# A transformer layer on one core: queries and keys turned in the q, k, v stage

## The reference

```python
mod = (silu(c) @ wmod).reshape(4, 6, 1, -1)        # sa, ca, ga, sb, cb, gb
h = layernorm(x) * (1 + ca) + sa
q = (layernorm(h) * qn_g + qn_b) @ Wq + bq          # k, v: the same with kvn_*, Wkv, bkv
q, k = rotary(q * hd**-0.25, |h|), rotary(k * hd**-0.25, |h|)
qn, kn = layernorm(q, ln_g, ln_b), layernorm(k, ln_g, ln_b)   # over the 32 channels of a head
w = softmax(causal(qn @ kn.T / sqrt(hd)))
x = x + ga * ((w @ v) @ Wo + bo)
x = x + gb * ffn(layernorm(x) * (1 + cb) + sb)
```

## Time and profile before

| | |
|---|---|
| three runs | 2335.0, 2336.63, 2336.87 us; median 2336.63 |
| the profiled execution | 2335.2 us, of which its span is 2333.5 |
| PE, DVE, ACT, POOL busy over the span | 93%, 51%, 34%, 32% |
| q, k, v stage | up to 399.7 us |
| attention | 399.7 to about 1100 us |
| PE's clock | full but for the starts of stages; mean 0.60 from 380 to 400 us, 0.5 at 400 to 460 us |
| chain that ended last | PE 45% of the span, all in the feed-forward stage |

### The profile page before, as it was taken

One profiled execution on the slowest core, in us unless ns is written; L12 is line 12 of the kernel. 1 busy time (PEld: TensorE's weight loads), 2 busy tenths in 40 slices (PEclk: granted clock), 3 DMA queues, 4 the chain that ended last, 5 costly groups with the idle time before them and its releaser, 6 DMA issues. The chain is left out here.

```text
span 2333.5 us, 36753 instructions
## 1 busy us (share of the span) xinstructions
PE 2167.5 (93%) x14056; PEld 1684.2 (72%) x14056; DVE 1190.7 (51%) x2747; ACT 788.2 (34%) x1575; POOL 758.3 (32%) x668
## 2 busy tenths in 40 slices
PE   6989995599999999998687999999999999999998
PEld 3777773377777777775465888888888888888887
DVE  5999996667667667663697122222211222222212
ACT  3333331066665666565355111111111111111111
POOL 2667776121222222222771222222222222222221
PEclk8999997599999999999898999999999999999999
DMA  6132322647575756641896112121111212121111
GB/s 235 58 105 90 108 94 102 154 108 167 127 164 127 165 139 152 152 103 39 261 308 216 54 55 68 50 68 36 60 64 50 68 55 68 50 73 50 53 33 54
DMA packets 164851, 243.99 MB, mean 105 GB/s; under 512 B 20604, under 2 KB 87292, under 8 KB 164184
## 3 DMA queue, kind: packets, MB, share of 16 engines
q1 hardware_dynamic: 160504, 229.27, 34.2%
q0 software_dynamic: 3136, 9.46, 1.3%
q10 hardware_dynamic: 1056, 3.15, 0.3%
HBM read 131.69 MB, written 59.26 MB: 82 GB/s over the span
## 5 line engine op out<-in xcount | busy, mean ns | idle before, releaser
L1363 DVE TENSOR_TENSOR f_gu<-f_psU,f_silu 128x512 f32<-128x512 f32 x128 | 88.5, 692 | 712.3 <-PE f_psU L1430 712.3
L999 ACT ACTIVATE b_probT<-b_psB 128x512 f32<-128x512 f32 (+1 forms) x640 | 316.8, 554 | 170.8 <-PE b_psB L863 168.5
L932 DVE TENSOR_REDUCE b_top<-b_psA 128x2 f32<-128x1024 f32 (+2 forms) x320 | 284.7, 902 | 153.8 <-PE b_psA L840 153.7
L1319 POOL TENSOR_SCALAR f_wd_hi<-f_wd 128x512 fp32r<-128x512 f32 x128 | 83.6, 653 | 823.8 <-PE f_psD L1415 776.2
L1339 ACT ACTIVATE f_silu<-f_psG 128x512 f32<-128x512 f32 x128 | 76.6, 598 | 504.4 <-PE f_psG L1430 504.4
L863 PEld LDWEIGHTS b_psB<-b_stack 98*128 98x128 f32 x1280 | 183.6, 190 | 73.1 <-issue 51.6
L863 PE MATMUL b_psB<-b_stack 98*128 98x256 f32 (+1 forms) x1280 | 218.3, 291 | 6.1 <-ACT b_probT L999 3.9
L1428 PE MATMUL f_psG<-f_hT_hi,w_hi 128*128 128x512 f32 x512 | 200.4, 391 | 11.4 <-DVE f_hT_lo L1357 11.4
L840 PE MATMUL b_psA<-b_stack 96*128 96x512 f32 (+3 forms) x768 | 184.7, 370 | 23.2 <-DMA b_stack<-b_halves 18.0
L1334 ACT ACTIVATE f_gu_hi<-f_gu 128x512 fp32r<-128x512 f32 x128 | 80.9, 632 | 364.5 <-DVE f_gu L1363 364.5
L1429 PE MATMUL f_psG<-f_hT_hi,w_lo 128*128 128x512 f32 x512 | 200.1, 391 | 0.0
(11 more groups left out here) (172 smaller groups left out, 4010.4 us busy)
## 6 DMA issues: line engine op xcount, KB each, us to landing
b_stack<-b_halves SPq DMA_DIRECT2D x192, 256.0 KB, 4.8
f_wd<-in_wd_t SPq DMA_DIRECT2D x128, 256.0 KB, 2.6
qkv_d<-a_t SPq DMA_DIRECT2D x32, 512.0 KB, 2.7
b_land<-qkv_d SPq DMA_DIRECT2D x32, 512.0 KB, 4.2
a_x<-in_x SPq DMA_DIRECT2D x32, 256.0 KB, 3.3
qkv_d<-a_v SPq DMA_DIRECT2D x32, 256.0 KB, 3.1
b_v<-qkv_d SPq DMA_DIRECT2D x16, 512.0 KB, 6.3
att_d<-b_acc SPq DMA_DIRECT2D x16, 512.0 KB, 3.2
```

The lines of the kernel that those rows point to most:

```text
L932: last = dve.tensor_reduce(into, tile[:, :, col:col + whole_blocks * P], AX.X, ALU.max, negate=True)
L999: act.activation(probT[:, (NW * n + w) % PROBS, j, 0:width], psB[:, i % BANKS, 0:width], ACT.Exp).then_inc(s["expd"], 1)
```

## The change

- After `norm_heads`, PE transposes a tile's queries and keys in the q, k, v stage (`turn_qk`, four blocks of 128 by 128 each, into `psT`), ACT scales and shifts them (`out_qk`), and SP stores them turned. `v` has two buffers in place of four, and is stored by itself. The eight small loads of `ln_g` and `ln_b` move into this stage.
- In attention, SP loads the turned rows straight into `whole`. `prepare`, `widen`, `land` and the slots of `psA` for them are gone. The load of the group after next stands behind the first three of the stack transfers, where it stood ahead of them.
- All lists of the stage are laid out by `in_turn`, without a loop. `product` is cut in three, and PE's order is product(0), `turn_h`, product(1), `turn_qk(0)`, product(2), `turn_qk(1)`. POOL has `norm_heads` first. The `pause` writes of this stage are plain waits.

```diff
+def in_turn(tiles, length, stages):
+    for u in range(tiles + max(lag for _, lag in stages)):
+        for stage, lag in stages:
+            if 0 <= u - lag < tiles:
+                stage(*divmod(u - lag, length))
...
-            stagger(sp, B, TB, [(load, 0), (store, 8)])
+            def store_v(b, t):
                 sp.wait_ge(s["v_ready"], done(b, t))
+                sp.dma_start(scratch["qkv"][b * TB + t, :, 2 * DM:], v[:, t % 2]).then_inc(v_stored[t % 2], 16)
+            def store_qk(b, t):
+                sp.wait_ge(s["qk_out"], twice(b, t, 2))
+                sp.dma_start(scratch["qkv"][b * TB + t, :, 0:2 * DM], qkT[:, t % 2].rearrange("p m n -> p (m n)")).then_inc(qk_stored[t % 2], 16)
+            in_turn(NT, TB, [(load, 0), (store_v, 6), (store_qk, 9)])
...
             def shift_x(b, t):
-                pause(nc, pool, spots[:, 4 + t % 4:5 + t % 4], still[:], s["scaled"], done(b, t))
+                pool.wait_ge(s["scaled"], done(b, t))
...
-            stagger(pool, B, TB, [(shift_x, 1), (norm_heads, 8), (rotate, 5), (centre, 6)])
+            in_turn(NT, TB, [(norm_heads, 8), (shift_x, 1), (rotate, 5), (centre, 6)])
...
-                pause(nc, dve, spots[:, 2:3], None, s["st1"], done(b, t))
+                dve.wait_ge(s["st1"], done(b, t))
...
-                at_least(dve, stored[t % 4], b * (32 * TB // 4) + 32 * (t // 4))
+                at_least(dve, s["qk_turned"], twice(b, t - 4, 2))
...
+            def out_qk(m):
+                def stage(b, t):
+                    if first(b, t, 0) and m == 0:
+                        act.wait_ge(s["ln_ready"], 1)
+                    if m == 0:
+                        at_least(act, qk_stored[t % 2], halved(b, t))
+                    act.wait_ge(s["qk_turned"], twice(b, t, m + 1))
+                    c = ln if m else ln_q
+                    act.activation(qkT[:, t % 2, m], psT[:, t % 2], ACT.Identity, scale=c[:, 0:1], bias=c[:, 1:2]).then_inc(s["qk_out"], 1)
+                return stage
+            in_turn(NT, TB, [(scale_x, 1), (high, 3), (root_h, 2), (root_x, 0), (take_v, 5), (square_h, 2),
+                             (square_heads, 6), (factor, 7), (out_qk(0), 8), (out_qk(1), 8)])
...
             def turn_h(b, t):
                 pe.wait_ge(s["hn_ready"], done(b, t))
                 at_least(pe, s["lo_ready"], done(b, t - 2))
+                at_least(pe, s["qk_out"], twice(b, t - 6, 2))
...
+            def turn_qk(m):
+                def stage(b, t):
+                    if m == 0:
+                        pe.wait_ge(s["qk_ready"], done(b, t))
+                        at_least(pe, s["qk_out"], twice(b, t - 2, 2))
+                    else:
+                        pe.wait_ge(s["qk_out"], twice(b, t, 1))
+                    for g in range(GROUPS):
+                        last = pe.transpose(psT[:, t % 2, g * P:(g + 1) * P], t2[:, t % 4, m * DM + g * P:m * DM + (g + 1) * P], ident[:])
+                    last.then_inc(s["qk_turned"], 1)
+                return stage
...
-            stagger(pe, B, TB, [(turn_h, 3), (product, 4)])
+            in_turn(NT, TB, [(product(0), 4), (turn_h, 3), (product(1), 4), (turn_qk(0), 8), (product(2), 4), (turn_qk(1), 8)])
...
             def load(n):
-                at_least(sp, s["turned"], 2 * n)
-                at = n % GROUPS * P
-                for m in (1, 0):
-                    sp.dma_start(land[:, m], rows_of(n)[:, :, at + m * DM:at + m * DM + P]).then_inc(s["qk_in"], 16)
+                at_least(sp, s["lo_done"], 2 * n)
+                for m in range(2):
+                    at = n % GROUPS * P + (1 - m) * DM
+                    sp.dma_start(whole[:, m].rearrange("p (t q) -> p t q", q=P), rows_of(n)[:, :, at:at + P]).then_inc(s["qk_in"], 16)
...
             def high(n, m):
-                pool.wait_ge(s["whole"], 2 * n + m + 1)
+                pool.wait_ge(s["qk_in"], 32 * n + 32)
```

More of the change, by code:

```diff
@@ L226, in load @@
                     sp.dma_start(sin_t[:], args["sin"].rearrange("(t p) d -> p t d", p=P)).then_inc(s["turn_in"], 16)
+                    for j in range(4):
+                        for n, name in enumerate(("ln_g", "ln_b")):
+                            sp.dma_start(ln[j * HD:(j + 1) * HD, n:n + 1], args[name].rearrange("(d a) -> d a", a=1)).then_inc(s["turn_in"], 16)
                 if first(b, t, 3):
@@ L254, in _ @@
                 sp.dma_start(scratch["mod"][:, m, :], late[at, n]).then_inc(late_out, 16)
-            for j in range(4):
-                sp.wait_ge(stored[j], 32 * NT // 4)
+            for j in range(2):
+                sp.wait_ge(v_stored[j], 16 * NT // 2)
+                sp.wait_ge(qk_stored[j], 16 * NT // 2)
             sp.wait_ge(late_out, 16 * 4)
@@ L358, in stat_h @@
                 dve.bn_stats(stats[:, t % 4, 1], h[:, t % 4]).then_inc(s["st2"], 1)
-                pause(nc, dve, spots[:, 3:4], None, s["st2"], done(b, t))
+                dve.wait_ge(s["st2"], done(b, t))
                 dve.bn_aggr(mv[:, t % 4, 1], stats[:, t % 4, 1]).then_inc(s["mv2"], 1)
@@ L409, in spread @@
                 dve.reciprocal(rec[:, t % 4], den[:, t % 4]).then_inc(s["rec_ready"], 1)
-            stagger(dve, B, TB, [(norm_h, 3), (norm_x, 1), (stat_h, 2), (stat_x, 0), (turn, 5), (low, 3), (means, 6), (spread, 7)])
+            in_turn(NT, TB, [(norm_h, 3), (norm_x, 1), (stat_h, 2), (stat_x, 0), (turn, 5), (low, 3), (means, 6), (spread, 7)])
             two = slice(0, B)
@@ L696, in slot_free @@
                 before, n = turns[at]
-                pe.wait_ge(s[{"score": "maxed", "prep": "whole", "peaks": "peaks_copied"}[before]], n + 1)
+                pe.wait_ge(s[{"score": "maxed", "peaks": "peaks_copied"}[before]], n + 1)
         @block.sync
@@ L763, in _ @@
                     lay_peaks(peaks_at(k))
-                if w == 4 and n + 2 < NG:
-                    load(n + 2)
                 if 0 <= n - 2 < NG - 1 and w in (3, 4, 6, 8):
@@ L769, in _ @@
                     lay_stacks(n + 1, w - 4)
+                if w == 4 and n + 2 < NG:
+                    load(n + 2)
                 if w == 7 and 0 <= n < NG:
@@ L817, in _ @@
             pe.wait_ge(s["ident_ready"], 2)
-            def prepare(n, m):
-                if m == 0:
-                    pe.wait_ge(s["qk_in"], 32 * n + 32)
-                slot_free(pe, "prep", 2 * n + m)
-                out = slot("prep", 2 * n + m).rearrange("p a w -> p (a w)")
-                for t in range(TB):
-                    mm = pe.transpose(out[:, t * P:(t + 1) * P], land[:, 1 - m, t], ident[:])
-                mm.then_inc(s["turned"], 1)
             def score(n, i):
@@ L899, in _ @@
                     weigh(*weigh_at(k), False)
-                if prep_at(k):
-                    prepare(*prep_at(k))
                 if peaks_at(k) is not None:
```

78 lines of the change are left out of this document (33 added, 45 removed).

## The result

The changed kernel takes 2347.56 us (median of 6 runs, 2343.69 to 2356.31), the kernel before beside it 2337.03 (6 runs, 2335.00 to 2339.21): ratio 1.0053, interval 1.0032 to 1.0073. The prediction said 2319 and a range of 2308 to 2346: the change costs half a per cent where I had it gain 0.8.

The account below looks back on a forecast made before the run. PE and DVE were taken as nearly full in the q, k, v stage, PE alone in attention. First stage +17.9 and attention -34.8 gave net -16.9 us: 2335.2 to 2318.3, predicted 2319 with the median's 1.4; range 2308 to 2346.

Parts of the forecast that it names:

- Attention's 27 transposes: Attention, PE-filled part: 27 `prepare`s of 1.14 us each go, -30.8 us (bounds 27.5 and 33.5).
- The failed step: Attention's fill: `load(1)` now stands among the first twelve stack transfers instead of ahead of them, costing 1 to 2.5 us.
- the fill: Start of attention, PE's clock low: three `prepare`s go, `load(1)` stands later; -4 us, between -8 and +1.
- third rival: Attention: ACT's exponentials, not PE, set the steps once transposes go; half the term lost, 2334 us; chance 0.04.
- second sign of being wrong: Attention: the prediction is wrong if attention ends less than 30 us sooner after its own start.
- The ring: q, k, v stage: new dependency loop through PE, ACT, POOL and DVE, 10.7 us a step, 24 x 0.05 = +1.2 us.
- second rival: q, k, v stage: `hmean` stays 0.8 us, the ring is 11.4 us, 24 x 0.7 = +17, 2336 us; chance 0.12.
- The race: q, k, v stage: DVE's `norm_x` starts 0.06 us ahead of POOL's `norm_heads` in every step; whoever starts first goes on.
- first rival: q, k, v stage: POOL's `norm_heads` starts first, `norm_x` waits; 24 steps x 1.85 are +44, 2363 us; chance 0.20.
- the start: q, k, v stage, first tile: `product(0)` ahead of `turn_h` lets PE work instead of waiting; -1.3 us, between 0 and -1.6.
- the last four steps: q, k, v stage: PE's added transposes are not hidden there, 41.9 against 37.4 us, +4.5 us.
- the end: End of q, k, v stage: late products with wmod come behind the last transposes, 8.7 us; +13.5 us (+11.5 to +19).

Follow-up runs that it names:

- experiment 2: Changed kernel with the attention's load tile `whole` doubled to two buffers and the load put ahead of all the stacks: 2316.85 us, 0.9914 of the kernel before.
- Experiment 6: Changed kernel with `out_qk(0)`, the copy of the queries, ahead of `square_heads` on ACT in the q, k, v stage: 2335.49 us, 0.9998 of the kernel before.
- Experiment 8: Changed kernel with a 64-column write (0.11 us) ahead of `norm_x` on DVE, so that it starts behind POOL's `norm_heads`: 2385.92 us, 1.0220 of the kernel before.
- 3: Changed kernel with the attention's load tile doubled, the load left between the first and second stack: 2345.80 us, 1.0035 of the kernel before.
- experiment 7: Changed kernel with the 32 late products laid in four parts of 8 between PE's last four q, k, v steps: 2343.95 us, 1.0030 of the kernel before.
- 12: Changed kernel with experiment 2, Experiment 6, experiment 7 (in three places, late copies and stores earlier) and `norm_heads` waiting for `norm_x`: 2294.33 us, 0.9819 of the kernel before.

## Why the prediction was wrong

**Attention's 27 transposes: the mechanism was right, its price was low, and it was eaten.** I had -30.8 between the marks, from 1.14 us a `prepare` with a bound of 33.5. Where nothing else is in the way (experiment 2) it is 600.8 - 562.8 = -38.0; 13 units have 2.74 us less each, 1.37 a `prepare`. By PE's starts 2.39 us of the 2.74 lie where the earlier trace rows has them, at the two `prepare`s. The other 0.35 are in the second group of shifted scores (L863) behind the second `prepare`: it took 0.85 us from its start to the next group's and takes 0.51 in experiment 2. Why it did stays open. The changed kernel got -17.2.

**The failed step is the load's.** The prediction priced the moved `load` only in the fill ("it was ahead of them: 1 to 2.5 us") and did not follow it past `few_out`, `load_v` and `wide_in`, in each of the 14 units. Its cost is the difference of the changed kernel and experiment 2: 20.8 us between the marks and 4.6 ahead of the first, 25 us in the two profiled executions. Going by the six traces of the changed attention it is 15 to 30 us between the marks, and the medians of the runs (2347.56 and 2316.85) are 30.7 apart. Since the transposes gave 7 more than I had, attention accounts for 18 of the 26 us by which the profiled execution misses the forecast's 2318.3; the first stage has 6.6, and the stages behind attention 1.5. The -4 of the fill was right (-4.2 with the load out of the way) and came to +0.3. That SP was the place, POOL's order the carrier and PE the one who waits was in none of the rivals. The third rival had the size (half the term lost) and the wrong cause: neither ACT nor DVE set the step, and with SP's order mended PE is full. The prediction's second sign of being wrong came true: attention's last mark comes 16.9 us sooner after its first load, and not 30. That experiment 2, at 2316.85 us, comes so near to the forecast of 2319 is luck: by its trace the first stage costs 7.4 us more than forecast, and attention gives 7.4 more.

**The ring: right in kind, mis-sized.** `hmean` fell to 0.18 us, which the second rival denied, but `out_qk(0)` took 0.76 us where I took `high`'s 0.58:
```profile
274.16 0.76 ACT L534 ACTIVATE a_qkT<-a_psT,a_ln_q 128x512 f32<-128x512 f32 x1
```
```profile
274.97 0.66 PE L589 MATMUL a_psT<-a_ident,a_t 128*128 128x128 f32 x4 [0.22 <-ACT a_qkT L534]
```
The step is 10.85 us and not 10.7: +3.4 in place of +1.2 over the 24. `high` was the wrong row to take. The same kind of operation, with a scale and a bias for each partition and out of PE's result tile, stood in the trace of before at two other widths, as `widen` and in the third stage:
```profile
L989 ACT ACTIVATE b_whole<-b_psA,b_ln x16: 1204/1206/1206, 411.2 to 990.8; 128x1024 f32<-128x1024 f32 x16
L1156 ACT ACTIVATE p_h<-p_psT,p_mod x128: 434/437/463, 1137.5 to 1269.9; 128x128 f32<-128x128 f32 x128
```
A straight line through 128 columns (0.437 us) and 1024 (1.206) gives an estimate of 0.77 us at 512; `out_qk` took 0.76 and 0.78. Experiment 6 shows that a place 2 us earlier on an idle ACT would have made the ring harmless.

**The race: as argued, won in all steps but one.** The margin is 0.08 us (forecast 0.06 to 0.07), and POOL pays for it; in the one step where DVE was 0.3 us late it was the other way:
```profile
274.25 0.75 DVE L371 SCALAR_TENSOR_TENSOR a_h<-a_x,a_mv,mod 128x512 f32<-128x512 f32 x1
...
186.37 2.18 DVE L371 SCALAR_TENSOR_TENSOR a_h<-a_x,a_mv,mod 128x512 f32<-128x512 f32 x1 [0.48 <-DVE a_rs L361]
```
```profile
274.33 2.45 POOL L312 TENSOR_TENSOR a_t<-a_t,a_fac 128x1024 f32<-128x1024 f32 x1 [1.38 <-ACT a_fac L523]
...
186.09 1.91 POOL L312 TENSOR_TENSOR a_t<-a_t,a_fac 128x1024 f32<-128x1024 f32 x1 [1.38 <-ACT a_fac L523]
```
That is +1.8. Experiment 8 gives the first rival's price: 1.43 us a step and 33 us over the 24 steps (38 in the medians), where I had 1.85 and 44. What the Trainium skill says (SBUF — State Buffer, "Who interferes with whom"), that the instruction that issues first keeps the shared ports for its whole length, agrees with both rows and with the experiment.

**The rest of the first stage:** the start -0.5 in place of -1.3 (tile 0 starts 1.6 us sooner, within the 2 us by which its start varies between traces, and the first three steps give 1.1 back); the last four steps +5.2 (4.5); the end +14.7 (13.5), of which the late products are 9.36 us where I took 8.7 (7.9 to 9.5 in the traces that have them as one block at the same place). With the ring and the race this makes +24.5 where I had +17.9.

## What to carry to other kernels

A DMA that is moved on its queue delays all that is issued behind it, in every round of the loop, in its issue and, here, in its landing too; follow the queue to the transfer that some engine waits for, and see what stands behind that engine's wait. Time taken off the bounding engine shortens the slack of every other chain in the same round, so each chain must be checked against the new length of the round. Price a wait of PE by the starts on both sides of it, not by the idle time that is listed. And take an operation's length from rows of the same operation, at other widths if need be, before one of the same width that does something else.

## What the runs showed of the hardware

- Issue times depend on what is in the queue: the two DMAs of the load took SP 1.06 us when it had been idle and 2.82 us directly behind three stacks.
- The load's place changes how long transfers take, not only when they are issued. Experiments 2 and 3 differ in the place alone: the median from issue to landing is 4.2 us with the load ahead of the stacks and 4.8 with it between them for the parts of `wide_in`, and 4.9 and 6.1 for the stacks.
- Where PE waits for late transfers, runs scatter more: 2343.7 to 2356.3 us (changed), 2331 to 2352 (experiment 7). Where it does not, it is 2316.4 to 2317.6 (experiment 2), 2293.4 to 2295.2 (12), five runs each, and 2332.1 to 2340.2 in 24 runs of the kernel before. The traces agree: one and the same attention program takes 577.8 to 592.7 us between the marks where PE waits, and two that are full repeat to 1.1 and 0.1 us. Why the transfers vary was not looked into.
- One ACT operation of 128x512 out of the same kind of tile takes 0.58 us as a plain copy (`high`) and 0.76 with a scale and a bias for each partition (`out_qk`). Which of the two makes the difference was not tried; one with a bias alone (L504 in the kernel before, 4x512, a single instance) took 0.68.
